# Two partitions instead of four between the last row pairs of even blocks, with two row stores instead of three in odd blocks

## What is computed

```python
r_feature: (2048, 200, 64) float32      L0_rec_weight: (200, 64, 64) float32
bilinear = jnp.einsum('bie,ied->bid', feature, weight)
out = jnp.einsum('bid,bjd->bij', bilinear, feature)      # (2048, 200, 200) float32, 327.68 MB
```

## Time and profile before

| | |
|---|---|
| median of 3 runs | 1420.39 us (1418.4 to 1421.25) |
| the profiled execution | 1419.37 us, span 1417.3 us |
| granted TensorE clock, mean | 0.997 |
| PE busy | 1379.1 us (97% of the span) |
| DVE, ACT, POOL busy | 986.8, 1016.3, 303.6 us |
| DMA | 438.60 MB, mean 309 GB/s |

### The profile page before, as it was taken

One profiled execution on the slowest core, in us unless ns is written; L12 is line 12 of the kernel. 1 busy time (PEld: TensorE's weight loads), 2 busy tenths in 40 slices (PEclk: granted clock), 3 DMA queues, 4 the chain that ended last, 5 costly groups with the idle time before them and its releaser, 6 DMA issues.

```text
span 1417.3 us, 40322 instructions
## 1 busy us (share of the span) xinstructions
PE 1379.1 (97%) x16192; PEld 1256.6 (89%) x16192; DVE 986.8 (70%) x1878; ACT 1016.3 (72%) x1100; POOL 303.6 (21%) x518
## 2 busy tenths in 40 slices
PE   7999999999999999999999999999999999999985
PEld 6899899999999899998999989999999998999964
DVE  0567677677776777667676677766777677676796
ACT  5687767777677776777668776777767776777753
POOL 0122222222222222222121222222222222122232
PEclk9999999999999999999999999999999999999998
DMA  9699999999999999999999989999999999999888
GB/s 274 215 296 305 317 329 312 309 301 321 335 306 323 301 324 316 328 300 305 334 324 304 318 283 331 329 300 321 317 331 318 309 306 313 317 321 315 269 303 300
DMA packets 268888, 438.60 MB, mean 309 GB/s; under 512 B 55712, under 2 KB 254368, under 8 KB 256416
## 3 DMA queue, kind: packets, MB, share of 16 engines
q1 hardware_dynamic: 244128, 422.80, 91.6%
q0 software_dynamic: 24576, 13.24, 3.6%
HBM read 108.13 MB, written 327.68 MB: 307 GB/s over the span
## 4 chain that ended last, share of the span: by engine, by line
PE 85%; DMA 6%; SPq 3%; DVE 3%; issue 2%; ACT 1%; POOLq 0%; ACTq 0%; POOL 0%; DVEq 0%
PE ps L311 47%; PE ps L295 25%; PE ps L283 13%; DMA out_dram<-staging 5%; SPq L225 2%; DMA x<-feature_dram 1%; DVE staging L348 1%; ACT staging L348 1%; DVE win L403 1%; SPq L211 1%; SPq L204 1%; DVE win L411 1%; DVE win L410 0%; ACT bl L373 0%; POOLq L88 0%
## 5 line engine op out<-in xcount | busy, mean ns | idle before, releaser
L311 PE MATMUL ps<-win,bl 64*109 64x200 f32 (+1 forms) x8192 | 808.2, 347 | 12.5 <-DVE staging L348 7.1
L311 PEld LDWEIGHTS ps<-win,bl 64*109 64x109 f32 (+1 forms) x8192 | 739.5, 232 | 58.9 <-issue 39.7
L348 ACT COPY staging<-ps 128x800 f32<-128x800 f32 (+1 forms) x683 | 540.4, 835 | 145.7 <-PE ps L311 100.2
L266 POOL DMA_DIRECT2D out_dram<-staging x512 | 302.9, 592 | 1104.4 <-ACT staging L348 881.0
L348 DVE COPY staging<-ps 128x800 f32<-128x800 f32 (+1 forms) x341 | 335.6, 984 | 196.3 <-PE ps L311 186.8
L373 ACT COPY bl<-ps 128x1024 f32<-128x1024 f32 (+1 forms) x208 | 301.6, 1451 | 167.6 <-PE ps L295 167.0
L403 DVE COPY win<-xt 128x400 f32<-128x400 f32 x512 | 275.4, 538 | 200.2 <-PE ps L311 152.7
L295 PE MATMUL ps<-xt,w 64*64 64x128 f32 x6400 | 392.8, 272 | 0.0
L295 PEld LDWEIGHTS ps<-xt,w 64*64 64x64 f32 x6400 | 344.4, 133 | 34.0 <-issue 33.9
L361 ACT COPY xt<-ps 128x1024 f32<-128x1024 f32 (+1 forms) x208 | 203.4, 981 | 69.6 <-PE ps L283 65.5
L283 PE MATMUL ps<-ident,x 128*128 128x128 f32 x1600 | 220.1, 281 | 14.3 <-DMA x<-feature_dram 10.3
## 6 DMA issues: line engine op xcount, KB each, us to landing
out_dram<-staging SPq DMA_DIRECT2D x512, 300.0 KB, 7.2
out_dram<-staging SPq DMA_DIRECT2D x768, 200.0 KB, 4.6
x<-feature_dram SPq DMA_DIRECT2D x80, 1024.0 KB, 8.8
x<-feature_dram SPq DMA_DIRECT2D x16, 1280.0 KB, 9.1
out_dram<-staging POOLq DMA_DIRECT2D x512, 25.0 KB, 5.4
w<-weight_dram SPq DMA_DIRECT2D x24, 128.0 KB, 6.1
w<-weight_dram SPq DMA_DIRECT2D x2, 64.0 KB, 3.8
```

What stands on the lines that cost most here:

```text
L266: nc.gpsimd.dma_start(out_v[FA:FH, PB * (s - 1):PB * (s + 1), :], staging[rest, slot - 1:slot + 1].rearrange("p s b h j -> p (s b) (h j)") ...
L311: last = nc.tensor.matmul(tile[0:top(s), h, F * b:F * (b + 1)], row_of_bl(n, R * k + PB * i + b)[64 * h:64 * h + 64], win[64 * h:64 * h + ...
L348: copy(staging[0:top(s), slot, :, :, :].rearrange("p b h j -> p h b j"), tile_of("scores", s)[0:top(s), :, 0:PB * F].rearrange("p h (b j) ...
```

## The change

In even blocks the last four pairs lie in columns 96, 98, 100 and 102, so that `TOP` is 103. In odd blocks a function `place_of` gives the column: pairs 0 to 63 lie two apart (0, 2, 4, ...), pairs 64 to 95 four apart from column 1, pairs 96 to 99 four apart from column 3. The odd blocks' three stores of 32 partitions become one of 64 and one of 32. Since the even blocks' third index follows the same places, ACT copies each weighed group of an even block in two halves (entries 0 to 63, then 64 to 127), the second counted by `bl_stored` and the first by a new semaphore `half_stored`; who waits for such a group waits for both.

```diff
-    TOP = FA + APART * (FH - FA - 1) + 1
+    TOP = FA + 2 * (FH - FA - 1) + 1
     LANES = NB // APART
+    WIDE = NB // 2
+
+    def place_of(m):
+        if m < WIDE:
+            return 2 * m
+        return APART * ((m - WIDE) % LANES) + 1 + 2 * ((m - WIDE) // LANES)
...
-        by_lane = bl[:].rearrange("p z (a d) -> p z d a", d=APART)
-
-        def group_of_bl(n, u):
+        by_half = bl[:].rearrange("p z (a d h) -> p z h a d", d=2, h=2)
+
+        def group_of_bl(n, u, half):
             if n % 2 == 0:
-                rows = slice(8 * u, 8 * u + GROUPS[u]) if 8 * u < FA else slice(FA, TOP, APART)
-                return bl[:, rows, :].rearrange("p c (a d) -> p c a d", d=APART)
-            first = 8 * u % LANES
-            return by_lane[:, :, 8 * u // LANES, first:first + GROUPS[u]]
+                rows = slice(8 * u, 8 * u + GROUPS[u]) if 8 * u < FA else slice(FA, TOP, 2)
+                return by_half[:, rows, half]
+            first = place_of(8 * u)
+            step = place_of(8 * u + 1) - first
+            return bl[:, :, first:first + step * (GROUPS[u] - 1) + 1:step]
...
-            return bl[:, 0:TOP, APART * (b % LANES) + b // LANES]
+            return bl[:, 0:TOP, place_of(b)]
...
+        def wait_bl(engine, at):
+
+            engine.wait_ge(bl_stored, at + 1)
+            n, u = at // NG, at % NG
+            if n % 2 == 0:
+                engine.wait_ge(half_stored, n // 2 * NG + u + 1)
...
-                for j in range(FA // LANES):
-                    sp.dma_start(out_v[LANES * j:LANES * (j + 1), PB * (s - 1):PB * (s + 1), :],
-                                 staging[j:NB:APART, slot - 1:slot + 1].rearrange("p s b h j -> p (s b) (h j)")
+                for rows, where in ((slice(0, WIDE), slice(0, NB, 2)), (slice(WIDE, FA), slice(1, NB, APART))):
+                    sp.dma_start(out_v[rows, PB * (s - 1):PB * (s + 1), :],
+                                 staging[where, slot - 1:slot + 1].rearrange("p s b h j -> p (s b) (h j)")
                                  ).then_inc(spread_written[slot // 2], 16)
...
-                rest = slice(FA, TOP, APART)
+                rest = slice(FA, TOP, 2)
                 if s // SETS_B % 2:
-                    rest = slice(FA // LANES, FA // LANES + APART * (FH - FA - 1) + 1, APART)
+                    rest = slice(place_of(FA), place_of(FH - 1) + 1, APART)
...
-                cells = "p (c d a) -> p c a d" if n % 2 == 0 else "p (c b) -> p b c"
...
-                sizes = {"d": APART, "a": LANES} if n % 2 == 0 else {"b": NB}
-                nc.scalar.copy(group_of_bl(n, u), weighed.rearrange(cells, **sizes)).then_inc(bl_stored, 1)
+                if n % 2:
+                    nc.scalar.copy(group_of_bl(n, u, 0), weighed.rearrange("p (c b) -> p b c", b=NB)
+                                   ).then_inc(bl_stored, 1)
+                else:
+                    first = weighed.rearrange("p (c h a d) -> p c h a d", h=2, d=2, a=LANES)[:, :, 0]
+                    other = weighed.rearrange("p (c h d a) -> p c h a d", h=2, d=2, a=LANES)[:, :, 1]
+                    nc.scalar.copy(group_of_bl(n, u, 0), first).then_inc(half_stored, 1)
+                    nc.scalar.copy(group_of_bl(n, u, 1), other).then_inc(bl_stored, 1)
```

More of the change, by code:

```diff
@@ L54, in feature_interaction @@
     assert 2 * E == 128 and B % NB == 0 and FH % 8 == C and R == 2 * PB
-    assert PB * F <= 512 and OSLOTS % 2 == 0 and TOP <= NB and FA % LANES == 0 and LANES % 8 == 0
+    assert PB * F <= 512 and OSLOTS % 2 == 0 and TOP <= NB and FA == WIDE + LANES and LANES % 8 == 0
     feature_v = feature.rearrange("b f e -> b (f e)")
@@ L114, in feature_interaction @@
         bl_stored = sem("bl_stored")
+        half_stored = sem("half_stored")
         own_filled = sem("own_filled")
@@ L191, in wait_tile @@
             elif before == "bilinear":
-                engine.wait_ge(bl_stored, then + 1)
+                wait_bl(engine, then)
             else:
@@ L247, in _ @@
                 if slot % 2:
-                    sp.wait_ge(spread_written[slot // 2], 16 * FA // LANES * stored(last, slot, 1))
+                    sp.wait_ge(spread_written[slot // 2], 32 * stored(last, slot, 1))
                     sp.wait_ge(rest_written[slot // 2], 16 * (stored(last, slot, 0) + stored(last, slot, 1)))
@@ L303, in scores @@
                 if k == 0 and i == 0:
-                    pe.wait_ge(bl_stored, (n + 1) * NG)
+                    wait_bl(pe, (n + 1) * NG - 1)
                 if i == 0:
@@ L343, in stage @@
                 if odd:
-                    engine.wait_ge(spread_written[slot // 2], 16 * FA // LANES * stored(before, slot, 1))
+                    engine.wait_ge(spread_written[slot // 2], 32 * stored(before, slot, 1))
                 else:
```

## The result

The changed kernel takes 1395.53 us (median of 4 runs, 1390.72 to 1398.49) against 1419.82 for the kernel before beside it (4 runs, 1418.4 to 1421.25): a ratio of 0.9833 [0.9814, 0.9852]. 1394.6 was forecast, within 1385 to 1410. The profiled execution took 1394.13 us with a span of 1392.3.

A forecast was written before the change was run, and what follows sets the result against it. PE (busy 1379.1 of 1417.3 us) was taken to bound the kernel, except at the program's ends. 1419.37 - 20.5 - 5.6 + 0.3 = 1393.6 for the profiled execution, 1.0 below the median: 1394.6 us, range 1385 to 1410.

The forecast's parts named there:

- 103 columns: Even blocks' score loads: six spread columns fewer at 1.67 ns save 10 ns a pair of records, -20.5 us.
- Faster copies of odd groups: ACT's copies into `bl` of odd blocks' first 64 pairs, now 8 bytes apart: taken as nothing, at best -2 us.
- Two stores: Odd blocks' stores: nothing while PE sets the pace; in the last block SP keeps up, -5.6 us at the end.
- The halves: ACT's copies of even blocks' weighed groups: 586 ns a half, 0.16 us more a group, +0.3 us before block 0.
- ACT's idle quarter: Odd blocks: ACT, busy 58.09 of 82.80 us, takes the halves' 2.1 us extra beside PE's scores.
- A: Even blocks: score spacing doesn't go by number of columns, so only the ends are won, 1415.1 us; chance 0.12.
- B: Even blocks: DMA takes back part, ACT waiting for slots; 1404.9 us with half lost, 1415.1 with all; chance 0.12.
- C: Even blocks: the spread load gets much cheaper and pairs reach 170 ns, 1374 us; chance 0.04.
- D: Odd blocks: halves 8 bytes apart cost like 16, 1.14 us more a group; 1447 us with half through; chance 0.04.

The follow-up runs named there:

- experiment 3: Changed kernel with each even block loading another number of spread columns (88 to 128), two blocks leaving out some scores: 1413.45 us in one run.
- experiment 1: Kernel before with only the even blocks' last four pairs two columns apart (103 columns), whole copies and three stores kept: 1407.63 us, ratio 0.9928.
- experiment 5: Changed kernel with ACT copying the weighed groups of the first 64 pairs of odd blocks twice: 1408.51 us, ratio 0.992.
- experiment 2: Changed kernel with the even blocks' last four pairs four columns apart again (109 columns), two stores and halves kept: 1411.04 us, ratio 0.9949.
- experiment 8: Changed kernel with POOL issuing the narrow stores in the last block and SP only the wide ones: 1394.89 us, ratio 0.9829.
- experiment 7: Changed kernel with three row stores of 32 partitions in odd blocks again: 1402.76 us, ratio 0.9878.
- experiment 6: Changed kernel with ACT copying both halves of even blocks' weighed groups twice (blocks 2 to 14): 1441.06 us, ratio 1.015.
- experiment 10: Changed kernel with even blocks loading only columns 0 to 99, stores unchanged, scores of their last two row pairs left out: 1389.93 us, ratio 0.9789.
- experiment 12: The changed kernel run once more as it is: 1396.48 us, ratio 0.9844.
- experiment 9: Changed kernel with the even blocks' last four pairs side by side, loads and stores of 100 columns: 1401.7 us, ratio 0.9877.
- experiment 11: Changed kernel with the last four pairs side by side (100 columns), twelve staging slots for 10, last load of x alone: 1395.17 us, ratio 0.9827.
- experiment 4: Changed kernel with even blocks' scores taking 103 columns from the weight tensor, 1 to 62 elements apart by block, weighed fields left out: 1404.02 us in one run.

## Why the prediction was right, and where its steps were not

**103 columns: right in the price, not in all that it needs.** -20.5 was forecast, at 1.67 ns a column; the load's price is 1.62 (experiment 3), pairs came 10 ns closer, and even blocks lost 21.1. The 1.4 ns at the lower end of the range had no row behind it. But alone the step is worth 12.4 (experiment 1). Most of the other 8.7 is the next step's.

**Faster copies of odd groups: the step that was mis-sized.** They were "taken as nothing; at best -2". They are worth 7.5 to 8.7 us beside the faster loads (experiment 1 against the change: 8.7 in even blocks, of which 7.5 at the sets that take over a group's tile), and copying those groups twice costs 14.9 in even blocks and 13.0 in all (experiment 5). I read the earlier trace rows, where PE hardly waits for copies into `bl`, as slack for good. It was slack at 190 ns a pair: four sets after a group PE wants its tile back, and the time it needs to get there shrinks with the loads. Experiments 5 and 1 show it from both sides; experiment 2 shows how little the copies are worth without the loads.

**Two stores: -5.6 forecast for the end, -2.8 measured.** The mechanism was right (SP's chain of issues is gone, DVE sets the pace of the last block, which kept its 61.7 us). Its size was off in two places: the last issue starts 3.0 us after the last matmul, not 1.6, since SP is still behind by a store then, and it takes 4.7 us to land, not 3.3. The DMA engines' share in the last block is 0.95 now, and experiment 8 says that an earlier issue would not have helped. "While PE sets the pace this changes nothing" was wrong too: beside the faster even blocks three stores cost some 4 us within the blocks (experiment 7, 7.2 less 2.8), where the waits for slots grew.

**The halves: right at their price, wrong in the reason.** 624 and 626 ns a half (block 3) for 586 forecast, and odd blocks did not lose. The reason given, ACT's idle quarter, falls with experiment 6: at 2.5 us a group 0.52 came through each time with ACT idle for a fifth. At 1.25 us a group the copy is done before PE wants the tile (odd blocks keep their pace), and that is what covers it. Before block 0 the halves cost +0.7 (47.1 to 47.8) for +0.3; in experiments 10 and 12 that piece is 47.0 and 46.6, so it varies by as much.

**The sum** was -25.8 and the span fell by 25.0: 2.8 too little at the end, and 0.4 too little before block 0, against 0.6 more in even blocks, 1.5 more in odd ones and 0.2 more in the last. That it is so near owes something to luck: the -20.5 came in full only because the step taken as nothing was part of the same change.

**The rivals.** A falls with experiment 3. B did not come with the change: even blocks lost their 21.1 us in full. Beyond it there is less room: experiments 9 and 10 shorten even blocks by 7.4 and 7.1 us, and odd ones take 10.7 and 2.7 more. But 2.7 is about the spread of odd blocks among runs that leave them and their stores as in the change (582.9 to 585.5 in experiments 2, 5, 8 and 12), and the 10.7 have a part of their own (experiment 10). C did not happen: 170 ns comes only with columns nearer than 16 bytes, or fewer than 100 of them. D's mechanism is real, and experiment 6 is its case, with a ratio above 1; its price did not come, because neighbours 8 bytes apart cost almost nothing extra (624 ns a half for 586).

**Open:** why the DMA packets of the last four pairs take longer from neighbouring partitions (experiments 9 and 11 against 10), and what limits experiment 11.

## What to carry to other kernels

Judge a copy by when its buffer is wanted back, not by the idle share of its engine; a list with few waits shows slack at today's pace only, so cost the parts of a change together. Where matmuls of one width and clock differ in pace, look at how far apart the columns of their weights lie. Read PE by the distances from start to start, since waits of a tenth of a microsecond stand in no list of waits.

## What the runs showed of the hardware that was not expected

- Loads of weights whose columns lie 4 elements (16 bytes) apart are slower than at 6, 16 and 32 elements (189 ns a pair against 181, 179 and 178), and 62 elements cost 196. At 1, 2 and 3 they stay at the floor of 170 to 171 (experiment 4). Why 4 and 62 stand out was not tried.
- After PE had stood still for 2.0 to 2.8 us in the middle of the scores, the granted clock was 0.50 (1.2 GHz) for 3.4 us, and 40 score records took 5.45 us for 3.60 (experiment 9; one such stretch each in experiments 4 and 7).
- The store of the last four pairs takes 4.8 to 5.4% of the DMA engines' span from four neighbouring partitions, and 3.6 to 4.0% from partitions two or four apart, at the same 13.24 MB (experiments 9 and 11 against the others).
- A store of 64 partitions is issued in the same 600 ns at the least as one of 32 (600 and 597), while the median from issue to landing is 5.7 us for the two sizes of the change against 4.6 with three stores of 32 (experiment 7).
